# A state-space stage of sixteen chunks: from a loop over pairs of chunks to sixteen chunks written out

## What is computed

```python
u, res = jnp.split(x @ W_in, 2, axis=-1)
u = silu(conv3(u))                                  # causal, three taps
dt, Bm, Cm = jnp.split(u @ W_x, [16, 32], axis=-1)
delta = softplus(dt @ W_dt + b_dt)                  # 512 channels
deltaA = exp(delta * A)                             # 16 states for each channel
deltaB_u = delta * u * Bm
h = deltaA * h + deltaB_u                           # along the 1024 tokens
y = sum over states of h * Cm, + u * D_param
y = (y * silu(res)) @ W_out
x = layernorm(x + y)
```

## Time and profile before

| | us |
|---|---|
| median of three runs | 2609.24 |
| lowest, highest | 2604.57, 2618.58 |
| the profiled execution | 2613.8 |
| its span in the trace | 2612.0 |
| state-space stage, to the last row statistics of number 16 | about 1709 |

### The profile page before, as it was taken

The page is one execution under the profiler, slowest core; times in us unless marked ns, Lnnn a source line. Parts: engine busy times, 40 slices in busy tenths (PEclk is TensorE's granted clock), DMA queues, the critical chain, the costliest instruction groups (busy, mean ns, idle before and its releaser), DMA issues. The chain is left out here.

```text
span 2612.0 us, 44554 instructions
## 1 busy us (share of the span) xinstructions
PE 2366.6 (91%) x14152; PEld 1840.0 (70%) x14152; DVE 2162.7 (83%) x2896; ACT 1748.6 (67%) x2984; POOL 1829.7 (70%) x932
## 2 busy tenths in 40 slices
PE   8999999999999999999999988656999999999995
PEld 3566666766766766666667666445988988988984
DVE  3899999999999999999999999976676566566565
ACT  3888889888888887898888898732334334334344
POOL 2698887987988988889889899532335525435457
PEclk9999999999999999999999999966999999999997
DMA  3211112212222212121122111112122312312353
GB/s 88 66 57 66 67 66 74 67 67 72 65 67 66 73 65 68 66 74 59 66 77 70 58 65 65 41 65 69 33 59 36 89 58 43 80 60 49 71 185 120
DMA packets 88281, 179.62 MB, mean 69 GB/s; under 512 B 8896, under 2 KB 51136, under 8 KB 88016
## 3 DMA queue, kind: packets, MB, share of 16 engines
q1 hardware_dynamic: 73136, 154.11, 17.9%
q0 software_dynamic: 14880, 22.29, 4.6%
HBM read 140.19 MB, written 36.18 MB: 68 GB/s over the span
## 5 line engine op out<-in xcount | busy, mean ns | idle before, releaser
L457 POOL TENSOR_TENSOR dbu<-du,b_all 128x2048 f32<-128x2048 f32 x255 | 1157.1, 4545 | 170.6 <-DVE hst L739 120.7
L550 ACT ACTIVATE da<-delta,a_neg 128x512 f32<-128x512 f32 x1008 | 691.5, 691 | 155.4 <-DVE hst L739 137.1
L739 DVE TENSOR_TENSOR_SCAN hst<-da,carry,dbu 128x512 f32<-128x512 f32 x504 | 618.4, 1266 | 29.5 <-ACT da L550 27.8
L739 DVE TENSOR_TENSOR_SCAN hst<-da,dbu 128x512 f32<-128x512 f32 x504 | 590.1, 1206 | 35.8 <-ACT da L550 28.6
L1952 PE MATMUL gu<-x_part,w_part 128*128 128x384 f32 (+1 forms) x2304 | 500.5, 366 | 10.0 <-issue 5.0
L1952 PEld LDWEIGHTS gu<-x_part,w_part 128*128 128x128 f32 x2304 | 415.0, 194 | 45.2 <-issue 12.4
L877 PE MATMUL hd<-ident,hst 128*128 128x128 f32 x2048 | 321.2, 279 | 80.0 <-DVE yacc L668 63.7
L668 DVE SCALAR_TENSOR_TENSOR yacc<-hd,c_tok,yacc 128x512 f32<-128x512 f32 x512 | 372.9, 728 | 23.6 <-PE hd L877 21.9
L877 PEld LDWEIGHTS hd<-ident,hst 128*128 128x128 f32 x2048 | 232.4, 141 | 224.8 <-issue 114.0
L877 PEld LDWEIGHTS w<-ident,hst 128*128 128x128 f32 x2048 | 239.3, 141 | 193.0 <-issue 101.0
L537 ACT ACTIVATE hTC<-w,c_tok 128x512 f32<-128x512 f32 x512 | 347.1, 678 | 24.7 <-PE w L877 24.1
(11 more groups left out here) (286 smaller groups left out, 2944.8 us busy)
## 6 DMA issues: line engine op xcount, KB each, us to landing
b_all<-b_rows SPq DMA_DIRECT2D x128, 512.0 KB, 3.7
xT<-in_xT SPq DMA_DIRECT2D x16, 514.0 KB, 5.0
xT_r<-in_xT SPq DMA_DIRECT2D x16, 512.0 KB, 4.9
x_rows<-in_x SPq DMA_DIRECT2D x16, 512.0 KB, 4.8
x_dram<-x SPq DMA_DIRECT2D x16, 512.0 KB, 3.0
acc_dram<-x SPq DMA_DIRECT2D x16, 512.0 KB, 4.4
w_raw<-in_wg SPq DMA_DIRECT2D x8, 1024.0 KB, 5.1
w_raw<-in_wu SPq DMA_DIRECT2D x8, 1024.0 KB, 7.7
```

Of the source, the lines that this page charges most:

```text
L457: nc.gpsimd.tensor_tensor(dbu[DBU[n]][:], du[parity][:], b_n, ALU.mult).then_inc(dbu_ready, 1)
L550: nc.scalar.activation(da_bank[t % 2][:], delta[parity][:, t, :], ACT.Exp, scale=a_neg[:, t, n:n + 1]).then_inc(da_ready, 1)
L739: nc.vector.tensor_tensor_scan(hst[DBU[n]][:, t, :], decay[:], dbu[DBU[n]][:, t, :], initial, ALU.mult, ALU.add).then_inc(scanned, 1)
```

## The change

The loop over six pairs is replaced by a Python loop that emits chunks 1 to 12 one after the other. Chunk numbers are now constants in all seventeen calls, and so are the values waited for and the addresses of the DMAs.

```diff
 def over_chunks(eng, emit):
 
     emit(Stage(0, 0, True, True, True, False))
-    with eng.Fori(0, (CHUNKS - 4) // 2) as i:
-        emit(Stage(i * 2 + 1, 1, True, True, True, True))
-        emit(Stage(i * 2 + 2, 0, True, True, True, True))
+    for c in range(1, CHUNKS - 3):
+        emit(Stage(c, c % 2, True, True, True, True))
     emit(Stage(CHUNKS - 3, 1, True, True, True, True))
     emit(Stage(CHUNKS - 2, 0, True, True, False, True))
     emit(Stage(CHUNKS - 1, 1, True, False, False, True))
```

## The result

The changed kernel took 2593.99 us (median of five runs, 2590.10 to 2599.09), where the kernel before had 2609.24 (2604.57 to 2618.58). The ratio is 0.9937, 95% interval 0.9914 to 0.9960: 0.63% less, 15 us by the medians. Timed again on another chip it was 0.9942 (0.9925 to 0.9958). The number on record was 2593.2. (Two single executions, of the kernel before and of the one with both loops written out, took 8211 and 5964 us; ratios and intervals leave such runs out.)

What follows compares the result with a forecast made beforehand. DVE was taken to bound the state-space stage, at about 97 us a chunk. Returns 13.8, constants 2.0 and entry 0.2 sum to 16.0 us, so 2609.24 becomes 2593.2 us (0.61% less), range 2581 to 2604.

Steps and rivals of the forecast that it cites:

- The bound and the place: State-space stage: DVE sets the pace, at least about 97 us a chunk; windows across the branch back are slower because DVE waits.
- Five returns, 13.8 us: Even-to-odd windows across the loop's branch back: each falls to 102.10 us, from 524.31 to 510.50 in all, 13.8 us gained.
- Constants for registers, 2.0 us: Waits in chunks 1 to 12 become waits on constants: 2.0 us gained, bounds nothing to 5 us.
- Entry 0.2 us, exit nothing: Start and end of the state-space loop: entering costs DVE 0.23 us, leaving nothing that shows; 0.2 us gained.
- Longer code, nothing: Twelve chunk bodies instead of two: fetching them costs nothing, at most 0.2 us a chunk, 2.4 us in all.
- The experts, nothing, from -3 to +4: Experts' loop, unchanged but further back: its two returns were taken to change nothing, with bounds of -3 to +4 us.
- the granted clock 1.00 in every window: Sign in the changed kernel's profile: PE's granted clock is 1.00 in every mark-to-mark window; before, three return windows had 0.98.
- pauses in "issue" of over 1 us inside chunks: Sign against the prediction: it is wrong if waits for a next instruction of over 1 us appear inside chunks.
- The pause did not come back as another wait: Rival at the returns: the pause goes, the time doesn't; only 2.2 us won, median 2607; chance 0.08.
- straight code did not stall: Rival in the twelve written-out chunks: fetching stalls, 2.8 us a chunk, 17 us slower, 2626 us; chance 0.04.
- more than the rows of chunk 13 said was won: Rival: 1.8 us more lost in all six even-to-odd windows, 11 us more, 27 in all, 2582 us; chance 0.05.

Runs made afterwards that it cites:

- the body of four chunks: Kernel before with four chunks per loop body instead of two, three rounds, so two returns instead of five; mark of chunk 13 at 1419.52 us, against 1426.48.

## Why the prediction was right

**The bound and the place.** Both held. DVE's own time in a window hardly changed (96.68 us against 97.09 and 96.85), and most of the gain came out of its gaps. Summed from the mark of chunk 1 to that of chunk 13 the windows are 16.4 us shorter and DVE is busy 3.3 us less, which the prediction had not counted apart.

**Five returns, 13.8 us.** The five windows sum to 509.41 us where they had 524.31: 14.9 us. The windows inside the body of four chunks, 102.12 us, split that: 5 x (104.86 - 102.12) = 13.7 us are the returns and 5 x (102.12 - 101.88) = 1.2 the registers. The mechanism stands on the runs: the slow windows move with the returns (four in the body), a return over a few instructions is free, one over 600 pauses and one over 300 does not. The two waits of DVE were read rightly as ACT's pause and PE's with its clock. Missed was that DVE pauses too, behind ACT, so that curing one engine alone would have left most of it: looping alone, ACT or DVE keeps 1.8 of the 3.0 us, and PE all; with PE alone cured 2.1 stay.

**Constants for registers, 2.0 us.** Six windows from odd to even fell from 607.28 to 605.97 us, 1.3 in all, as counted (1.2). For the even to odd ones the term was 0.14 us each and is 0.24 (five of them), and chunk 12 to 13 fell from 102.10 to 101.91. Together 1.3 + 1.2 + 0.2 = 2.7 us against 2.0. It is ACT's registers (0.16 from odd to even) more than DVE's (0.05), and not PE's (0.00).

**Entry 0.2 us, exit nothing.** The mark of chunk 1 is 0.67 us earlier (192.79 to 192.12), but between executions of the same code that mark itself lies at 192.12 and 190.60. The last four scans of chunk 0 tell the term: from the scan of slot 60 to the first of chunk 1 it took 6.09 us (to 160.82) and takes 5.80, 0.29 less. First the kernel before, then the changed one:

```profile
154.73 2.34 DVE L739 TENSOR_TENSOR_SCAN hst<-da,dbu 128x512 f32<-128x512 f32 x2 [0.74 <-ACT da L550]
```
```profile
154.40 2.34 DVE L738 TENSOR_TENSOR_SCAN hst<-da,dbu 128x512 f32<-128x512 f32 x2 [0.77 <-ACT da L549]
...
160.20 2.46 DVE L738 TENSOR_TENSOR_SCAN hst<-da,carry,dbu 128x512 f32<-128x512 f32 x2
```

All five profiles in which DVE loops have 6.09 to 6.11 us there, all nine others 5.80 or 5.81. So the term is 0.3 us, and 0.33 of the 0.67 lies ahead of it in chunk 0, where no code changed. Leaving the loop shows nothing beyond the registers.

**Longer code, nothing.** In chunks 1 to 13 it cost nothing that can be read: 101.00 and 101.88 us in all windows. The instruction queues moved less than in the earlier trace rows, not more:

```profile
q8 instruction: 119, 1.95, 0.3%
q14 instruction: 92, 0.75, 0.1%
```

2.70 MB for 40,340 instructions is 67 bytes for each, 3.22 for 44,554 was 72. The reading that the loop was fetched anew in every round fits. It fits one engine at a time, too: with PE alone looping q8 moves 2.10 MB as before the change, with PE written out 1.93 to 1.97 (as long as the loop over the experts stays), and a loop kept on the core would have moved far less, not more.

**The experts, nothing, from -3 to +4.** 904.98 against 905.01 us. At the two returns of their loop PE's weight loads now pause 1.67 and 1.91 us, where the earlier trace rows had 1.50 and 1.46.

**The sum.** 16.0 us was the forecast and 15.0 the span's difference: 17.1 won and 2.1 given back. Of the 17.1, 0.3 are the start of chunk 0; the change itself won 13.7 + 2.7 + 0.3 = 16.7 us. The given-back part had no term, and the sign "the granted clock 1.00 in every window" failed by it. It is a low piece of PE's clock in chunk 14, which six of the ten profiles with PE written out have, so the closeness of 16.0 to 15.0 owes something to an accident: in the other profile of the changed kernel it isn't there, and chunks 1 to 16 are 1514.20 - 1497.97 = 16.2 us shorter than before, against 14.3 in the first. One more of the signs has to be answered, pauses in "issue" of over 1 us inside chunks. The first profile has one:

```profile
1538.14 0.72 PEld L876 LDWEIGHTS hd<-ident,hst 128*128 128x128 f32 x4 [0.68 <-DVE yacc L667]
...
1541.19 0.71 PEld L876 LDWEIGHTS w<-ident,hst 128*128 128x128 f32 x4 [1.50 <-issue]
```

The loads are at 0.72 us, the lower clock, before the pause, and the second profile has neither. So it goes with the clock and is no stall of the longer code.

**The rivals.** The pause did not come back as another wait; straight code did not stall; more than the rows of chunk 13 said was won only by 0.2 us a window, not 1.8. Of the 1.1 us by which an even to odd window is longer, 0.9 stay in straight code (101.88 against 101.00), so they are no cost of the loop; what they are is open.

## What to carry to other kernels

Look for a stretch of the loop's body that is also written out somewhere, in the lead-in or the tail, and measure mark to mark on the engine that sets the pace: the difference is what a return costs, before anything is tried. A return paused here where the body was long (478 instructions and more on DVE, not 300; 359 on ACT either way), and it does so on each engine for itself, side by side; so either write out all the long streams, or put more work in the body. Add to the pause what may follow it: after some of PE's pauses of 3 us its clock was at the lower level, and that nearly doubled what they cost (1.6 us without, 3.05 on average).

## What the runs showed of the hardware

- The pause at a return over a long body, as the views show it, is 2.5 to 3.2 us on ACT, 2.6 to 3.5 on PE's matmuls, and 3.54 on DVE with short instructions; behind scans of 1.2 us, which are queued ahead, only 1.6 of it shows on DVE.
- From the branch to the loop's head it took 0.24 to 0.29 us on POOL and SP with 121 and 71 instructions in a round, and 2.8 to 3.3 on DVE with 478. ACT with 359 took 0.25 us in two profiles and about 3 in ten, with the same body.
- A loop's own branch, taken over a few instructions or falling through, changed no window of this stage by more than 0.04 us. Between short memsets on DVE a return over 100 or 300 instructions took 0.35 to 0.39 us.
- DVE stops 0.32 us after every 128 short instructions of straight code, and no such gap shows in a body of 300 or 100 that is repeated.
- PE's granted clock fell in some windows after a pause of about 3 us and not in others, with the same code: 103.52 us at 1.00 after 3.38 us, and 106.45 us at 0.97 after 3.03.
